# A graph layer, a linear-attention mixer and eight experts in one program: the last graph product and the expert layer taken in two halves of rows

## The reference

```python
h = relu(graph_conv(h, W_rel2, b_rel2, W_root2) @ W_lin2.T + b_lin2)   # graph_conv: agg @ W_rel.T + b + h @ W_root.T
x = x + h + mixer(xn)
xf = layernorm(x)                                # (v + 1e-5) under the root, 1024 x 512
logits = xf @ router_w                           # 512 x 8
gate_vals, idx = top_k(logits, 2); gates = softmax(gate_vals)
for e in range(8):                               # hidden width 32, eps 1e-6
    hid = relu(xf @ w1[e] + b1[e]) @ w2[e] + b2[e]
    out += where(idx == e, gates, 0).sum(-1)[:, None] * (normalise(xf + hid) * gamma[e] + beta[e])
return x + out
```

## Time and profile before

| | |
|---|---|
| runs, us | 1174.13, 1172.45, 1168.41; median 1172.45 |
| profiled execution, us | 1172.11, its span 1170.3 |
| mean granted TensorE clock | 0.975 |
| busy, us (share of the span) | PE 1095.2 (94%), PEld 881.6 (75%), DVE 702.9 (60%), ACT 363.3 (31%), POOL 155.6 (13%) |
| chain that ended last, by engine | PE 79%, DVE 11%, issue 4%, ACT 4%, POOL 1% |

### The profile page before, as it was taken

One profiled execution on the slowest core, in us unless ns is written; L12 is line 12 of the kernel. 1 busy time (PEld: TensorE's weight loads), 2 busy tenths in 40 slices (PEclk: granted clock), 3 DMA queues, 4 the chain that ended last, 5 costly groups with the idle time before them and its releaser, 6 DMA issues.

```text
span 1170.3 us, 15993 instructions
## 1 busy us (share of the span) xinstructions
PE 1095.2 (94%) x5936; PEld 881.6 (75%) x5952; DVE 702.9 (60%) x1545; ACT 363.3 (31%) x648; POOL 155.6 (13%) x126
## 2 busy tenths in 40 slices
PE   3989799999999999999999999999999999998895
PEld 3767798987777777777898877777778888887431
DVE  7565677479675667467664488756644135028566
ACT  4234466525221301125665334131210011011212
POOL 4230202000000001201001000000003420600016
PEclk9998999999999999998999999999999999999896
DMA  6220101003321112000101004111526210000001
GB/s 210 105 91 1 37 2 37 1 5 100 81 63 46 55 46 77 1 1 4 35 1 38 6 18 136 45 55 45 220 64 220 73 28 10 17 19 1 1 9 64
DMA packets 34798, 60.42 MB, mean 52 GB/s; under 512 B 19456, under 2 KB 20416, under 8 KB 34080
## 3 DMA queue, kind: packets, MB, share of 16 engines
q1 hardware_dynamic: 12352, 40.23, 10.8%
q10 hardware_dynamic: 22368, 19.11, 5.1%
HBM read 48.85 MB, written 10.49 MB: 51 GB/s over the span
## 4 chain that ended last, share of the span: by engine, by line
PE 79%; DVE 11%; issue 4%; ACT 4%; POOL 1%; DMA 0%; POOLq 0%; ACTq 0%; DVEq 0%
PE ps_a L494 10%; PE ps_a L495 9%; PE ps_a L496 9%; PE ps_v L494 8%; PE ps_v L495 8%; PE ps_v L496 8%; PE ps_a L768 5%; PE ps_v L685 4%; PE ps_v L871 3%; PE ps_v L696 3%; PE ps_a L515 3%; PE ps_a L620 2%; PE ps_a L599 2%; DVE expk L1414 2%; DVE stats L1280 1%
## 5 line engine op out<-in xcount | busy, mean ns | idle before, releaser
L494 PE MATMUL ps_a<-ht_hi,w_hi 128*128 128x512 f32 x496 | 197.3, 398 | 1.7 <-DVE headmask_r L1379 0.9
L495 PE MATMUL ps_a<-ht_lo,w_hi 128*128 128x512 f32 x496 | 194.5, 392 | 0.0
L496 PE MATMUL ps_a<-ht_hi,w_lo 128*128 128x512 f32 x496 | 194.4, 392 | 0.0
L896 ACT ACTIVATE work<-ps_a,col_sb 128x512 f32<-128x512 f32 x96 | 66.7, 719 | 203.1 <-PE ps_a L496 145.2
L494 PEld LDWEIGHTS ps_a<-ht_hi,w_hi 128*128 128x128 f32 x496 | 93.9, 189 | 25.0 <-DVE headmask_r L1379 1.3
L496 PEld LDWEIGHTS ps_a<-ht_hi,w_lo 128*128 128x128 f32 x496 | 93.9, 189 | 20.3
L495 PEld LDWEIGHTS ps_a<-ht_lo,w_hi 128*128 128x128 f32 x496 | 94.1, 190 | 19.5
L1533 DVE TENSOR_TENSOR xm<-ps_v,xm 128x512 f32<-128x512 f32 x80 | 55.2, 690 | 86.0 <-PE ps_v L496 85.5
L494 PE MATMUL ps_v<-w_hi,f_hi 128*128 128x512 f32 x256 | 101.8, 398 | 0.0
L496 PE MATMUL ps_v<-w_hi,f_lo 128*128 128x512 f32 x256 | 99.8, 390 | 0.0
L495 PE MATMUL ps_v<-w_lo,f_hi 128*128 128x512 f32 x256 | 99.7, 390 | 0.0
(11 more groups left out here) (206 smaller groups left out, 1987.3 us busy)
## 6 DMA issues: line engine op xcount, KB each, us to landing
stage<-wstream SPq DMA_DIRECT2D x62, 512.0 KB, 3.7
adj_d<-adj_win ACTq DMA_DIRECT2D x16, 256.0 KB, 2.9
adj<-adj_d ACTq DMA_DIRECT2D x2, 2048.0 KB, 12.1
xt_d<-xt_hi SPq DMA_DIRECT2D x2, 1024.0 KB, 5.0
xt_d<-xt_lo SPq DMA_DIRECT2D x1, 2048.0 KB, 11.4
ht_hi<-xt_d ACTq DMA_DIRECT2D x1, 2048.0 KB, 8.0
ht_lo<-xt_d ACTq DMA_DIRECT2D x1, 2048.0 KB, 12.9
x_again<-x ACTq DMA_DIRECT2D x8, 256.0 KB, 9.2
```

The source lines that it names most:

```text
L494: nc.tensor.matmul(ps, left[0], right[0], start=first, stop=False)
L495: nc.tensor.matmul(ps, left[0], right[1], start=False, stop=False)
L496: return nc.tensor.matmul(ps, left[1], right[0], start=False, stop=last)
L896: nc.scalar.activation(work[:, n % 4, :], psA[:, i % BANKS, :], func, **how).then_inc(a_empty, 1)
```

## The change

Half 0 (tiles 0 to 3) of stages 2 to 5 is carried out among half 1's. Two tables, `TAIL_A` and `TAIL_V`, number the results of the whole tail in the two rings. On TensorE four W_lin2 products come behind the first convolution block of half 1, and half 0's turn ahead of the last one; half 0's router, choice, masks, first layer and second layer come between half 1's W_lin2 products, turn, router and choice. Each half has its own choice (`choose(h)`, four tiles) and its own masks. A tile's scaling is now one tile behind its second layer.

The bias b_lin2 is no longer added on VectorE: a thirteenth matmul at the head of each product (`lin_sel`, 32 rows) puts it into the bank. The turned half is copied to its high part by ScalarE, straight from PSUM, and VectorE's subtraction reads PSUM too. ScalarE copies the turned hot rows.

W2 and b2 have their mean over the 512 output features subtracted on chip (`prepare_experts`, VectorE), so that `z`, a sum of a normalised row and a centred one, has no mean left. The statistics of `z` become one ScalarE pass with a square and its sum (`square`). POOL turns it into the scale, per tile: an addition of eps, a power with exponent -1/2, a product with the gate (`scale`). VectorE applies scale and gamma in one step (`weigh`). The shift and the scaled copy `ut` are gone. POOL adds as before (`add_pair`, `add_experts`), but for the last tile, where VectorE does it. The small rows are split on VectorE and not POOL; their loads and W2's stand on SP's queue, behind the last weight piece. POOL splits W_lin2 one product earlier.

The core of the diff; `choose(h)`, left out, holds the steps of before for four tiles:

```diff
+TAIL_V = numbered(
+    [("lin", t) for t in range(5)] + [("logits", 0)] + [("lin", t) for t in range(5, NT)]
...
+    + [("z", 0, NT - 1)] + scales(NT - 2) + [("z", 1, NT - 1)] + scales(NT - 1)
+)
...
+            sp.wait_ge(w_split, N_SLOTS * PIECES)
+            sp.dma_start(small_sb[:], small).then_inc(small_in, 16)
+            sp.dma_start(w2_sb[:], w2).then_inc(small_in, 16)
+            sp.dma_start(repl[:], repl_c).then_inc(small_in, 16)
...
+            def lin(t):
+                if t % HALF_NT == 0:
+                    pe.wait_ge(split, LAYERS * 16 - 16 + done(SP_G + t + 3))
+                ps = tail_bank("lin", t)
+                nc.tensor.matmul(ps, lin_sel[:], small_r[0:SET, 1, :], start=True, stop=False)
+                for k in range(KT):
+                    last = mm3(ps, part(hT, k, nodes(t % HALF_NT)), weight(2, k), False, k == KT - 1)
+                last.then_inc(v_full, 1)
...
+            conv(1, 0)
             pe.wait_ge(w_split, N_SLOTS * PIECES)
-            for t in range(NT):
...
-                into_nat(slot_of(2), hT, t, bank_v(GV_X + t)).then_inc(v_full, 1)
-                if t == NT - 3:
-                    turn_experts_input(0)
...
+            pe.wait_ge(small_ready, 1)
+            for t in range(HALF_NT):
+                lin(t)
+            conv(1, 1)
+            conv(1, 2)
+            turn_experts_input(0)
+            conv(1, 3)
+            route(0)
+            lin(4)
+            turn_logits(0)
+            for t in range(5, NT):
+                lin(t)
+            turn_hots(0)
+            spread_hots(0)
             hidden(0)
             turn_experts_input(1)
-            route(0)
+            second_layer(0, 0)
+            second_layer(1, 0)
             route(1)
...
+            second_layer(0, 1)
+            turn_logits(1)
+            second_layer(1, 1)
+            pick_scales(0)
+            second_layer(0, 2)
+            second_layer(1, 2)
             hidden(1)
...
+            def high_turned(h):
+                for k in range(KT):
+                    i = TA + TAIL_A["turn", h, k]
+                    act.wait_ge(a_full, i + 1)
+                    nc.scalar.activation(xfT[h][0][:, k, :], psA[:, i % BANKS, :], ACT.Copy).then_inc(turn_high, 1)
...
+            def take_hots(h):
+                i = TV + TAIL_V["hot", h]
+                act.wait_ge(v_full, i + 1)
+                act.wait_ge(v_empty, done(i - 1))
+                nc.scalar.activation(hotT[:, half(h)], psV[0:3 * SET, i % BANKS, :], ACT.Copy).then_inc(v_empty, 1)
...
+            def square(t):
...
-                    nc.scalar.activation(ut[t % 2][:, q, :], zz[q][:, t, :], ACT.Identity, scale=gscale[:, column],
-                                         bias=gshift[:, column]).then_inc(shifted, 1)
+                    taken_v(act, "z", q, t)
+                    n = 2 * t + q
+                    column = slice(n, n + 1)
+                    if n >= 4:
+                        act.wait_ge(squared, n - 3)
+                    nc.scalar.activation(work[:, n % 4, :], zz[q][:, t % HALF_NT, :], ACT.Square, scale=D ** -0.5,
+                                         accum_out=square_mean[:, column]).then_inc(squared, 1)
...
+            def scale(t, first, last):
+                columns = slice(2 * t + first, 2 * t + last)
+                pool.wait_ge(squared, 2 * t + last)
+                nc.gpsimd.tensor_scalar(square_mean[:, columns], square_mean[:, columns], EPS_MOE, None,
+                                        ALU.add).then_inc(square_eps, last - first)
+                pool.wait_ge(square_eps, 2 * t + last)
+                nc.gpsimd.tensor_tensor(gscale[:, columns], square_mean[:, columns], nhalf[:, columns],
+                                        ALU.pow).then_inc(square_root, last - first)
+                pool.wait_ge(square_root, 2 * t + last)
+                nc.gpsimd.tensor_tensor(gscale[:, columns], gscale[:, columns], gate[:, 2 + first:2 + last, t],
+                                        ALU.mult).then_inc(scale_ready, last - first)
+            def add_pair(t):
+                taken_v(pool, "gamma", 1, t)
+                both = weighted[t % 4]
+                nc.gpsimd.tensor_tensor(both[:, 0, :], both[:, 0, :], both[:, 1, :], ALU.add).then_inc(pair_summed, 1)
...
+            def low_turned(h):
...
+                    dve.wait_ge(turn_high, h * KT + k + 1)
+                    nc.vector.tensor_tensor(xfT[h][1][:, k, :], psA[:, (TA + TAIL_A["turn", h, k]) % BANKS, :],
+                                            xfT[h][0][:, k, :].bitcast(f32), ALU.subtract).then_inc(a_empty, 1)
...
-                nc.vector.tensor_tensor(lin_sum[:, t % 2, :], psV[:, i % BANKS, :], lin_row[:], ALU.add).then_inc(v_empty, 1)
...
+            def onto_graph(t):
+                ps = tail_job("lin", t)
+                nc.vector.scalar_tensor_tensor(out=Xm[:, t, :], in0=ps, scalar=0.0, in1=Xm[:, t, :], op0=ALU.max,
+                                               op1=ALU.add).then_inc(v_empty, 1)
+                taken_v(dve, "lin", t)
                 statistics(residual, [t])
...
+                for m in range(2):
+                    nc.vector.bn_stats(w2_stats[:, m, :], w2_sb[:, m, :])
+                then(nc.vector.bn_stats(w2_stats[second, 2, :], small_sb[second, 0, :]))
...
+                for m in range(2):
+                    nc.vector.tensor_scalar(w2_sb[:, m, :], w2_sb[:, m, :], w2_mean[:, m, 0:1], None, ALU.subtract)
+                then(nc.vector.tensor_scalar(small_sb[second, 0, :], small_sb[second, 0, :], w2_mean[second, 2, 0:1], None,
+                                             ALU.subtract))
...
+                then(nc.vector.tensor_copy(small_r[:], small_sb[:]))
+                then(nc.vector.tensor_tensor(small_sb[:], small_sb[:], small_r[:].bitcast(f32), ALU.subtract))
+                then(nc.vector.tensor_scalar(small_sb[:], small_sb[:], high_rows[:, 1:2], None, ALU.mult))
+                nc.vector.scalar_tensor_tensor(out=small_r[:], in0=small_r[:].bitcast(f32), scalar=high_rows[:, 0:1],
+                                               in1=small_sb[:], op0=ALU.mult, op1=ALU.add).then_inc(small_ready, 1)
...
+            def weigh(q, t):
+                column = slice(2 * t + q, 2 * t + q + 1)
+                ps = tail_job("gamma", q, t)
+                dve.wait_ge(scale_ready, 2 * t + q + 1)
+                nc.vector.scalar_tensor_tensor(out=weighted[t % 4][:, q, :], in0=zz[q][:, t % HALF_NT, :],
+                                               scalar=gscale[:, column], in1=ps, op0=ALU.mult, op1=ALU.mult).then_inc(v_empty, 1)
...
+            prepare_experts()
+            dve.wait_ge(a_full, TA + KT)
+            for m in range(KT):
+                split_conv(0, m)
+            dve.wait_ge(x_added, NT)
+            for t in range(HALF_NT):
+                onto_graph(t)
+            normalise_experts(0)
+            for m in range(KT - 1):
+                split_conv(1, m)
+            low_turned(0)
+            split_conv(1, KT - 1)
+            nc.vector.memset(hot[:], 0.0)
+            onto_graph(4)
+            choose(0)
+            for t in range(5, NT):
+                onto_graph(t)
+            normalise_experts(1)
+            mask_hidden(0)
+            low_turned(1)
+            add_z(0, 0)
+            add_z(1, 0)
+            add_z(0, 1)
+            choose(1)
+            add_z(1, 1)
+            take_scales(0)
+            add_z(0, 2)
+            add_z(1, 2)
+            take_scales(1)
+            mask_hidden(1)
+            for t in range(3, NT - 1):
+                add_z(0, t)
+                add_z(1, t)
+                take_scales(t - 1)
+            last = NT - 1
+            add_z(0, last)
+            take_scales(last - 1)
+            add_z(1, last)
+            add_shift(last)
+            dve.wait_ge(summed, last - 3)
...
-                    nc.vector.tensor_tensor(zz[q][:, t, :], ps, Xf[:, t, :], ALU.add).then_inc(v_empty, 1)
-                    if q == 1:
-                        expert_done(dve, "z", 1, t)
-                        statistics(lambda c: zz[c % 2][:, t, :], range(2 * t, 2 * t + 2), NT)
...
-                    nc.vector.tensor_tensor(weighted[t % 2][:, q, :], ps, ut[t % 2][:, q, :], ALU.mult).then_inc(v_empty, 1)
...
+                weigh(q, last)
+                taken_v(dve, "gamma", q, last)
+                if q:
+                    dve.wait_ge(last_added, 1)
+                nc.vector.tensor_tensor(Xm[:, last, :], weighted[last % 4][:, q, :], Xm[:, last, :],
+                                        ALU.add).then_inc(last_summed if q else last_added, 1)
```

More of the change, by code:

```diff
@@ L358, in build @@
+        weighted = [at(f"weighted{n}", [P, 2, D], f32, "slots", 8 * KB + 4 * KB * (n % 2) + 32 * KB * (n // 2)) for n in range(4)]
         psA = ctx.enter_context(nc.psum_tensor("ps_a", [P, BANKS, 512], f32))
@@ L805, in _ @@
-            x0 = SLOTS - 1
```

(34 more changed lines are left out.)

575 lines of the change are left out of this document (286 added, 289 removed).

## The result

The changed kernel takes 1162.7 us (median of 8 runs, 1160.23 to 1167.84) against 1171.2 for the kernel before in the same sessions: a ratio of 0.993, 95% interval 0.9905 to 0.9955. So it is faster by 0.7%, a little more than the 0.5% that a measurement here can tell. The profiled execution took 1162.99 us (span 1161.2, mean granted clock 0.983); that of before took 1172.11.

The account below looks back on a forecast made before the run. TensorE was taken to bound the kernel until a 21.6 us tail of waits. Last product at 1145.8 plus tail 7.5 gave span 1153.3, time 1155.1; 8.4 of slow clock made 1163.5, say 1163, range 1153 to 1172.

Parts of the forecast that it names:

- signs of a wrong mechanism: Tail over 10 us, last product after 1150 at full clock, or the clock falling in the convolution or lin products.
- The tail: From the last second-layer product to the end: 7.5 us (7.2 to 8.3) instead of 21.6, saving 14.1.
- rival 4: The tail stays because POOL's additions for tile 6 and their store are late; at worst 2 us; no chance given.
- The bias: Thirteenth matmul in each of eight lin products, 0.227 us each: 1.8 us added, bounds 1.8 and 3.4.
- The waits of the new order: TensorE's added waits of 1.0, 1.0, 0.4, 2.3 and 1.8, sum 6.5 us; five tile-to-tile waits stay, 2.8.
- The clock: Half clock falls twice in the second layer, two slow products each, costing 8.4 us together.
- third stretch: TensorE around half 1's turned hot rows and masks, about 4.0 us: clock falls, two slow products, 4.2 us.
- the second: TensorE behind choose(1), about 3.5 us with small matmuls: clock falls, two slow products, 4.2 us.
- Edits at nothing: Centring W2, splitting small rows (about 12 us on VectorE) and splitting W_lin2 earlier have cover and cost no time.
- Up to half 0's end: Half 0 of the last graph convolution ends at 1023.7 us as before; nothing the diff touches moves it.
- the first (one brief fall): Rival: the clock holds, or falls once and briefly, giving 1155 us; chance 0.2.
- The third's crowding of POOL: Rival: halves cost more waits, POOL's in-order queue becomes the bound, some 6 us on top, 1169; chance 0.13.

Follow-up runs that it names:

- Experiment 1: Changed kernel with the bias matmul of each W_lin2 product over 128 rows (zero rows added) instead of 32; 1160.57 us, ratio 0.9925 to the kernel before.
- experiment 4: Changed kernel without its halves, keeping bias matmul, centred W2, mean square and scaling per tile; 1159.78 us, ratio 0.9921 to the kernel before.
- experiment 2: Changed kernel with POOL's split of W_lin2 put back behind the second graph layer's first product; 1165.49 us, ratio 0.9951 to the kernel before.
- experiment 6: Changed kernel with eleven unread 8-row matmuls in TensorE's waits around half 1's masks; 1164.09 us, ratio 0.9925 to the kernel before.
- experiment 5: Changed kernel with eleven unread dense matmuls in TensorE's waits around half 1's masks; 1159.1 us, ratio 0.9897 to the kernel before.
- experiment 7: Changed kernel without halves, with 128-row bias matmul, late W_lin2 split and second-layer results in the ps_a ring; 1150.96 us, ratio 0.9816 to the kernel before.
- experiment 8: Kernel without halves, with 128-row bias, late split and second-layer results in ps_a, plus unread dense matmuls around the masks; 1151.9 us, ratio 0.9813 to the kernel before.

## Why the prediction was right in size, and where its steps were not

The forecast of 1163 met 1162.7 (1162.99 in the profiled execution), but several of its terms were off. Half 0 of the convolution ended 3.7 later than forecast, the part from there to the last product took 2.8 more at full clock (124.9 for 122.1), and the slow clock took 6.7 less (1.7 for 8.4). That these cancel is luck. One of the prediction's own signs of a wrong mechanism came true: at full clock TensorE's last product ends at 1154.0 - 1.7 = 1152.3, later than 1150. Counted from half 0's end as forecast it would be 1148.6.

**The tail: right.** 14.1 forecast, 14.4 measured. From the last addition of `z` on, the path is the forecast one: ScalarE's square (0.63 and an accumulator read of 0.18, forecast 1.0), three POOL steps, and two VectorE steps. The power on one column takes 0.57, forecast 0.6 by the slope between four columns and eight. The profile's chain nevertheless stays on POOL from 1149.17 on, since POOL's addition for tile 6 ends at 1155.63 (1154.41 + 1.22), just behind ScalarE's read:

```profile
1155.33 0.18 ACT L1174 ACTIVATION_READ_ACCUMULATOR work<-z 128x1 f32 x1
1155.72 0.22 POOL L1326 TENSOR_SCALAR square_mean<-square_mean 128x1 f32<-128x1 f32 x1
```

So the addition that rival 4 names is as late as the path itself, and costs at most 0.1 us here. No experiment takes the edits of the tail apart (scaling by tile, the mean square in place of the statistics, the last tile added on VectorE).

**The bias: mis-sized, outside its bounds.** "I take the dense one, as its neighbours are dense": 1.8, upper bound 3.4. Among dense matmuls it cost 0.65 a product. Experiment 1 took 2.6 off the part, so that the eight cost 1.8 + 2.6 = 4.4. The bound was the row of a small matmul itself, 0.43; it left out that the small matmul starts late and that the next dense ones do too.

**The waits of the new order: right in place, 1.8 too small.** Forecast 1.0, 1.0, 0.4, 2.3, 1.8 and five of 0.55; the trace has 0.93 (and one of 0.20 beside it), 1.04, 0.35, 2.48, 2.9 (2.19 and 0.71), and five of 0.64. Together 11.1 for 9.3. choose(1) took 3.85 (forecast 4.2), and the long idle stood where it was put. The one that missed is the masks' wait: behind ScalarE's copy, VectorE's masking is late too.

**The masks: a saving that the forecast left out.** With 2.6 more for the bias, 1.8 more for the waits and 0.3 more for work that was put down to the slow clock, the forecast 122.1 would have become 126.8, against 124.9 measured. Of the 1.9 between them 1.7 stand at the masks. TensorE's second four masks before, then the first four now:

```profile
1099.30 2.49 PE L861 MATMUL ps_v<-hot_t,repl_r 8*128 8x512 f32 x4 [0.52 <-DVE hm L1749]
```
```profile
1086.77 0.74 PE L822 MATMUL ps_v<-hot_t,repl_r 8*128 8x512 f32 x4 [1.04 <-ACT hot_t L1158]
```

Before, the second four have to wait for VectorE to free the four banks of the first; now each half needs only four. The eight masks keep TensorE busy for 1.5 us instead of 3.2. The kernel of experiment 4, without halves, has 2.49 there again. The forecast took the busy time of before as work that stays, and part of it was this wait. This is what the halves did save; their other waits cost more.

**The clock: mechanism partly right, number wrong.** Forecast two falls with two slow products each, 8.4 us. The profiled execution had one, behind the second masks, with one slow product: 3.45 + 0.58 instead of 1.91 + 0.43, 1.7 us. The fall at choose(1) did not come there: the clock stood at 1.00 from 1108 to 1110 with TensorE busy 0.64 of 2 us. In the profiles of experiments 2 and 6 both falls came. Five profiles have this wait at 2.48 or 2.49 (changed, experiments 1, 2, 5, 6), and two of them the fall behind it. So the third stretch was rightly held alike to the one before 1100.5, while the second was like it only at times. What was also wrong is to forecast a number of slow products for one execution: behind the masks the same code had one in the changed kernel's profile and two in experiment 1's. Experiments 5 and 6 support the part of the argument that set thin work apart from dense.

**"Edits at nothing": one failed.** I looked for cover of W_lin2's split in TensorE's timeline and not in VectorE's beside POOL; it cost 1.1 us (experiment 2). The collision was in the trace of before too, at another place, in rows I had not read: a cast of 2.61 at 956.84 beside a POOL subtraction of 2.71. The other edits kept their cover: the preparation of W2 and the small rows took VectorE 8 us (1003.69 to 1011.8; estimate 12) and left 15.85 idle before split_conv(0,0).

**Up to half 0's end: 3.7 late instead of 0.** Of this 1.1 is the split. The other 2.6 are there before it, in code that the change leaves alone and that got other stretches at half clock (from 560 to 580 us a granted clock of 0.88 now and 1.00 before); no experiment separates them.

So -14.4 + 5.9 - 4.3 + 3.7 stands for the forecast's -14.1 + 3.4 + 2.1. The idea behind the change was half right: experiment 4 shows that the new scaling, with the edits that go with it, gives the gain, and that cutting the work into halves gives none. Of the rivals, the first (one brief fall) describes the profiled execution's second layer, though not its time of 1155. The third's crowding of POOL is at the edge in the tail of the changed kernel, and costs 1.6 us in experiment 7, once TensorE had become faster.

## What to carry to other kernels

Split a gain by mechanism before keeping all of a change: here a reordering that by the rows cost 2.4 us rode along with a rescaling that saved 14. Give a small bias matmul among dense ones as many rows as its neighbours have, and read POOL's rows beside VectorE's before moving a POOL step "beside idle time". When a product waits for the bank it writes, look for banks of another ring that have no more use: here that removed seven waits of 0.64. Before counting a row's busy time as work, see whether its matmuls stand in it waiting for banks.

## What the runs showed of the hardware that was not expected

- A 32-row matmul among 128-row ones made three starts late: 0.32, 0.42 and 0.34 us, where neighbours with equal rows start 0.22 apart (experiment 1).
- A VectorE cast of 0.42 took 2.61, and a subtraction of 0.69 took 1.41, while POOL cast and subtracted in SBUF (experiment 2).
- With its waits filled by 8-row matmuls TensorE was granted 0.77 and then 0.50 (experiment 6, one profile), with dense ones 1.00 (experiments 5 and 8).
- Half clock came in different stretches of the same code in the profiles (620 to 640 us: 0.91, 1.00 and 0.71); the runs of the changed kernel lie between 1160.23 and 1167.84.
